# Four chained adaLN blocks on one core: how the first group's bias reaches the Vector engine, and where the later biases are computed

## What is computed

```python
h = gelu(embedding @ W0 + b0); h = gelu(h @ W1 + b1)
att   = softmax(h @ W2 + b2)                       # 64 x 8
agg_w = einsum('bk,koi->boi', att, weight)         # a 32 x 32 matrix for each sample
agg_b = att @ bias_k                               # 64 x 32: the bias
cond  = einsum('boi,bih->boh', agg_w, x) + agg_b[:, :, None]
ffn   = (silu(cond @ W_gate.T) * (cond @ W_up.T)) @ W_down.T      # 512 -> 1792 -> 512
```

## Time and profile before

| what | us |
|---|---|
| median of 3 runs | 540.56 |
| lowest, highest | 539.83, 541.33 |
| the profiled execution, its own time | 541.38 |
| its span (first to last instruction) | 539.5 |
| PE busy in the span | 528.5 (98%) |
| DVE, ACT, POOL busy | 236.1, 140.7, 153.8 |

### The profile page before, as it was taken

How to read it: one execution, slowest core, us unless ns; L and a number is a source line. 1 busy time by engine, 2 the same in 40 slices (tenths; PEclk the granted TensorE clock), 3 DMA queues, 4 the chain that set the end, 5 groups by cost and what they waited for, 6 DMA issues and landing times.

```text
span 539.5 us, 6961 instructions
## 1 busy us (share of the span) xinstructions
PE 528.5 (98%) x2643; PEld 392.4 (73%) x2643; DVE 236.1 (44%) x537; ACT 140.7 (26%) x247; POOL 153.8 (29%) x153
## 2 busy tenths in 40 slices
PE   7999999999999999999999999999999999989997
PEld 6888888888888888888888886635454544567885
DVE  3432343622223623233522334544525257887665
ACT  5422222322222322222222222000002217545333
POOL 3399994400000400000300930040002000127556
PEclk9999999999999999999999999999999999999999
DMA  8298540295000230000305000959696919589763
GB/s 298 98 416 319 176 103 0 74 146 111 0 0 0 85 90 0 0 0 0 94 6 137 1 1 0 149 130 160 198 190 176 229 26 224 110 167 195 186 137 137
DMA packets 82502, 61.60 MB, mean 114 GB/s; under 512 B 61744, under 2 KB 66864, under 8 KB 81712
## 3 DMA queue, kind: packets, MB, share of 16 engines
q1 hardware_dynamic: 77696, 41.83, 35.2%
q0 software_dynamic: 4704, 19.40, 14.2%
q10 hardware_dynamic: 80, 0.08, 0.0%
HBM read 38.98 MB, written 12.81 MB: 96 GB/s over the span
## 4 chain that ended last, share of the span: by engine, by line
PE 94%; DVE 3%; ACT 1%; DMA 1%; issue 0%; POOL 0%; DVEq 0%; POOLq 0%
PE ps L673 93%; DVE cT L1368 1%; DMA pack_a<-in_pack_a 1%; ACT c_hi L1069 0%; PE ps L873 0%; PE ps L834 0%; DVE xs L1194 0%; DVE rest L1385 0%; PE ps L988 0%; PE ps L887 0%; DVE wcat L1391 0%; DVE m L1381 0%; POOL silu L568 0%; DVE cT L1194 0%; DVE stat L1394 0%
## 5 line engine op out<-in xcount | busy, mean ns | idle before, releaser
L673 PE MATMUL ps<-c_hi,wl 128*128 128x512 f32 x448 | 169.9, 389 | 0.0
L673 PE MATMUL ps<-c_lo,wl 128*128 128x512 f32 x448 | 169.7, 389 | 0.0
L1194 DVE TENSOR_TENSOR hff<-silu,ps 128x512 f32<-128x512 f32 x56 | 38.5, 687 | 164.7 <-PE ps L673 164.7
L673 PEld LDWEIGHTS ps<-c_lo,wl 128*128 128x128 f32 x448 | 84.1, 188 | 17.4
L673 PEld LDWEIGHTS ps<-c_hi,wl 128*128 128x128 f32 x448 | 84.0, 188 | 17.4
L673 PE MATMUL ps<-wl,h_hi 128*128 128x512 f32 x224 | 87.7, 391 | 0.0
L673 PE MATMUL ps<-wl,h_lo 128*128 128x512 f32 x224 | 87.2, 389 | 0.0
L1103 ACT ACTIVATE silu<-ps 128x512 f32<-128x512 f32 x56 | 33.5, 598 | 118.6 <-PE ps L673 118.6
L1194 DVE TENSOR_TENSOR h_lo<-hff,h_hi 128x512 fp32r<-128x512 f32 x56 | 46.8, 836 | 39.1 <-ACT h_hi L1069 39.1
L1069 ACT ACTIVATE h_hi<-hff 128x512 fp32r<-128x512 f32 x56 | 35.4, 632 | 108.8 <-DVE hff L1194 108.8
L673 PE MATMUL ps<-wbase,cT 128*128 128x512 f32 x128 | 56.4, 594 | 0.0
(11 more groups left out here) (184 smaller groups left out, 568.3 us busy)
## 6 DMA issues: line engine op xcount, KB each, us to landing
wl<-in_wl POOLq DMA_DIRECT2D x14, 768.0 KB, 8.5
stg<-y_dram SPq DMA_DIRECT2D x64, 128.0 KB, 5.0
xs<-in_x SPq DMA_DIRECT2D x4, 1024.0 KB, 8.2
x_all<-in_x SPq DMA_DIRECT2D x1, 4096.0 KB, 13.7
y_dram<-prod SPq DMA_DIRECT2D x16, 256.0 KB, 2.2
x_dram<-x_all SPq DMA_DIRECT2D x4, 1024.0 KB, 7.0
x_all<-cS POOLq DMA_DIRECT2D x4, 1024.0 KB, 7.6
x_all<-in_bias POOLq DMA_DIRECT2D x4, 1024.0 KB, 10.8
```

What stands on the lines that cost most here:

```text
L673: return pe.matmul(o, l, r, start=start, stop=stop)
L1194: return dve.tensor_tensor(o, a, b, op)
```

## The change

The transpose of the first attention is taken from `att[:, 0]` (64 x 8) as soon as it is normalised, ahead of the three masked products; a small product with `kbias[0:8]` (8 rows, 32 columns) gives the bias of all 64 samples for block 0; ACT copies it to `btab[:, 0]`; SP writes its first 16 rows to a DRAM tensor, waits, and reads them back broadcast into `bias_bc`. Gone are the transpose of `att_m[:, 0]`, the copy to `attT[:, 0]`, `terms`, the wide product and the copy to `bias_bc`, and two of five filler products. POOL issues weight slices 0 and 1 at once, and 2 and 3 after `bias_bc` has landed. The other biases (block 1: 2 matmul instructions; blocks 2 and 3: 4; the bias by rows: 8) move from behind the 16 products to three places inside `gate_up(0, 0)`, ahead of the high pairs of chunks 0, 1 and 2. `gate_up(0, 0)` stands ahead of the loop, and `gate_up(g + 1, 0)` at the end of the loop's body; each group's matmuls and their order stay.

```diff
# SP
+            sp.wait_ge(s_btab0, 1)
+            sp.dma_start(bias0_dram, btab[0:GB, 0]).then_inc(s_bias0_dram, 16)
+            sp.wait_ge(s_bias0_dram, 16)
+            sp.dma_start(bias_bc[:], bias0_dram.rearrange("b o -> (b o)").unsqueeze(0).broadcast_to([P, TOK])).then_inc(s_bias_bc[0], 16)
             sp.wait_ge(s_btab, 2)
             sp.dma_start(bias_dram, btab[:]).then_inc(s_bias_dram, 16)
# POOL
-            weights(0, 3)
+            weights(0, 2)
             pool.wait_ge(s_pack_c, 16)
-            pool.wait_ge(s_attT, 1)
-            pool.tensor_tensor(terms.rearrange("p (b o) -> p b o", o=ROWS),
-                               attT[:, 0, 0:GB].unsqueeze(2).broadcast_to([P, GB, ROWS]),
-                               kbias[:, 0:ROWS].unsqueeze(1).broadcast_to([P, GB, ROWS]), ALU.mult).then_inc(s_terms, 1)
+            pool.wait_ge(s_bias_bc[0], 16)
+            weights(2, 4)
             split_c(0)
-            weights(3, 4)
             pool.wait_ge(s_h_lo, 1)
             weights(4, M)
# PE
             pe.wait_ge(s_set, 2)
-            for n in range(5):
+            for n in range(3):
                 mm(bank(7)[:, 0:P], ones[:], ones[:])
+            pe.wait_ge(s_pack_c, 16)
+            pe.wait_ge(s_att, 6)
+            pe.transpose(bank(0)[0:K, 0:NB], att[:, 0], ident[0:NB, 0:NB]).then_inc(s_first_turned, 1)
             pe.wait_ge(s_att, 7)
             mm(bank(3)[:, 0:NT * K], selrep, att_m[:, 0]).then_inc(s_att_spread, 1)
-            pe.wait_ge(s_pack_c, 16)
-            pe.transpose(bank(0)[:, 0:NB], att_m[:, 0], ident[0:NB, 0:NB]).then_inc(s_att_turned, 1)
+            pe.wait_ge(s_att_first, 1)
+            mm(bank(0)[0:NB, P:P + ROWS], att_first, kbias[0:K, 0:ROWS]).then_inc(s_bias0, 1)
...
-            pe.wait_ge(s_terms, 1)
-            mm(bank(0), ones[:], terms).then_inc(s_bias0, 1)
...
                 if m == 0:
                     for s in range(S):
+                        ahead(s)
                         pe.wait_ge(s_c_hi, S * g + s + 1)
...
             def layer0(g, more):
-                for m in range(M):
+                for m in range(1, M):
                     gate_up(g, m)
-                    if m >= 1 and (more or m < M - 1):
+                    if more or m < M - 1:
                         down(g, m - 1)
...
-            pe.wait_ge(s_attT, 2)
-            for l, i in COND.items():
-                mm(bank(1)[0:NB, l * ROWS:(l + 1) * ROWS], attT[:, i], kbias[:, i * ROWS:(i + 1) * ROWS])
-            mm(bank(1)[0:NB, ROWS:2 * ROWS], condT, cwT)
-            for b in range(TB):
-                ins = mm(bank(1)[b * ROWS:(b + 1) * ROWS, P:P + NT], ...)
-            ins.then_inc(s_bias_mm, 1)
+            pe.wait_ge(s_attT, 1)
+            def later_bias(s):
+                if s == 0:
+                    mm(bank(1)[0:NB, ROWS:2 * ROWS], condT, cwT)
+                elif s == 1:
+                    for l in (2, 3):
+                        i = COND[l]
+                        mm(bank(1)[0:NB, l * ROWS:(l + 1) * ROWS], attT[:, i], kbias[:, i * ROWS:(i + 1) * ROWS])
+                elif s == 2:
+                    for b in range(TB):
+                        ins = mm(bank(1)[b * ROWS:(b + 1) * ROWS, P:P + NT], ...)
+                    ins.then_inc(s_bias_mm, 1)
+            gate_up(0, 0, later_bias)
             with pe.Fori(0, G - 1) as g:
                 layer0(g, True)
+                gate_up(g + 1, 0)
             layer0(G - 1, False)
# ACT
+            act.wait_ge(s_first_turned, 1)
+            copy(att_first, bank(0)[0:K, 0:NB]).then_inc(s_att_first, 1)
+            act.wait_ge(s_bias0, 1)
+            copy(btab[:, 0], bank(0)[0:NB, P:P + ROWS]).then_inc(s_btab0, 1)
             act.wait_ge(s_att_turned, 1)
-            copy(attT[:, 0], bank(0)[:, 0:NB]).then_inc(s_attT, 1)
-            act.wait_ge(s_att_turned, 2)
             copy(attT[:, 1:3].rearrange("p i n -> p (i n)"), bank(1)[:, 0:2 * NB]).then_inc(s_attT, 1)
             act.activation(scrap[:], scrap[:], ACT.Silu)
-            act.wait_ge(s_bias0, 1)
-            copy(bias_bc[:], bank(0)).then_inc(s_bias_bc[0], 16)
```

More of the change, by code:

```diff
@@ L171, in build @@
         bias_dram = nc.dram_tensor("bias_dram", (NB, 4, ROWS), F32).ap()
+        bias0_dram = nc.dram_tensor("bias0_dram", (GB, ROWS), F32).ap()
         ps = ctx.enter_context(nc.psum_tensor("ps", [P, 8, 512], F32))
@@ L213, in cT3 @@
             return xs if g % 2 else cT
-        terms = silu[:, 0]
+        att_first = silu[0:K, 0, 0:NB]
         prod0 = hff[:].rearrange("p b (j k o) -> p (b j) k o", k=K, o=ROWS)
@@ L242, in build @@
         s_attT = sem("s_attT")
-        s_terms = sem("s_terms")
+        s_first_turned = sem("s_first_turned")
+        s_att_first = sem("s_att_first")
         s_bias0 = sem("s_bias0")
+        s_btab0 = sem("s_btab0")
+        s_bias0_dram = sem("s_bias0_dram")
         s_mix0 = sem("s_mix0")
@@ L726, in cond, with gate_up @@
                     cond_chunk(l, g, s, b)
-            def gate_up(g, m):
+            def gate_up(g, m, ahead=lambda s: None):
                 n = g * M + m
@@ L804, in _ @@
                         ins.then_inc(s_cond_mm[0], 1)
-            pe.wait_ge(s_attT, 2)
-            for l, i in COND.items():
-                mm(bank(1)[0:NB, l * ROWS:(l + 1) * ROWS], attT[:, i], kbias[:, i * ROWS:(i + 1) * ROWS])
-            mm(bank(1)[0:NB, ROWS:2 * ROWS], condT, cwT)
-            for b in range(TB):
-                ins = mm(bank(1)[b * ROWS:(b + 1) * ROWS, P:P + NT], kbias[:, COND[2] * ROWS:(COND[2] + 1) * ROWS],
-                         attT[:, COND[2]].rearrange("p (t b) -> p b t", b=TB)[:, b])
-            ins.then_inc(s_bias_mm, 1)
+            pe.wait_ge(s_attT, 1)
[8 more added lines that the diff above has]
+                    for b in range(TB):
+                        ins = mm(bank(1)[b * ROWS:(b + 1) * ROWS, P:P + NT], kbias[:, COND[2] * ROWS:(COND[2] + 1) * ROWS],
+                                 attT[:, COND[2]].rearrange("p (t b) -> p b t", b=TB)[:, b])
+                    ins.then_inc(s_bias_mm, 1)
+            gate_up(0, 0, later_bias)
             with pe.Fori(0, G - 1) as g:
                 layer0(g, True)
+                gate_up(g + 1, 0)
             layer0(G - 1, False)
@@ L1110, in _ @@
             act.wait_ge(s_bias_mm, 1)
-            copy(btab[:].rearrange("b l o -> b (l o)"), bank(1)[0:NB, 0:4 * ROWS]).then_inc(s_btab, 1)
+            copy(btab[:, 1:4].rearrange("b l o -> b (l o)"), bank(1)[0:NB, ROWS:4 * ROWS]).then_inc(s_btab, 1)
             copy(biasN, bank(1)[:, P:P + NT]).then_inc(s_biasN, 1)
```

## The result

The changed kernel is slower: a median of 542.50 us over 19 runs against 541.51 of the kernel before over 19 runs beside it, a ratio of 1.0019 with a 95% interval of 1.0013 to 1.0026. That is 1.0 us where 0.4 less was forecast. It lies inside what the prediction called no change (0.3%), but the interval over 19 runs leaves out 1, and the sign is not the one that was forecast. The median of before in that comparison is 0.95 above the three runs known ahead, so differences count here, not absolute times.

A forecast was written before the change was run, and what follows sets the result against it. The prediction took PE's chain through the beginning, up to gate_up(0, 0), as the bound. An earlier chunk 0 (-0.6) and the moved biases (+0.2) gave -0.4 us, median 540.56 to 540.2, range 539.0 to 542.1.

The forecast's parts named there:

- no change (0.3%): Whole kernel: 0.3%, 1.6 us, can't be told from no change; a result within that had a chance of 0.82.
- PE's path through the beginning: Before 19.2 us: PE's waits decide; any gain or loss reaches the end of block 0, 330.8, unchanged.
- The fillers' step: PE's beginning: four fewer filler instructions end 0.85 us earlier; the spreading product starts at 9.30, all DVE work 0.25 earlier.
- The loop's edge at 0: gate_up(g + 1, 0) ahead of the loop's jump: priced 0, bounds -0.1 and +0.3 us for three edges.
- 22.57: Forecast time at which gate_up(0, 0) is through (slice 1's first product): 16.67 + 5.9, against 22.98 before.
- The profiled execution would take 541.38 - 0.4: Whole kernel: the profiled execution falls to 540.98 us, the median from 540.56 to 540.2.
- The 0.6 of chunk 0 (16.57): The 16 xs products: chunk 0 complete at 16.57, so DVE adds the bias at 16.67, not 17.27, 0.6 us earlier.
- The first rival: Clock rises later: all 32 instructions of the 16 products run low, +1.35 us, up to 2 more; median 542.1; chance 0.12.
- I take 3.0 and 2.6: it lands at 16.3: Bias by DRAM: store 3.0 us, load 2.6, landing at 16.3 against 16.6 when DVE asks, slack 0.3 us.
- I estimate 0.3 for a visit: Each of three later-bias places inside gate_up(0, 0): 0.3 us, plus 0.06 per instruction and 0.07 for the last 8.
- 5.9: From DVE's first addition to the end of gate_up(0, 0): 5.9 us with the moved biases, against 5.7 before.
- A rule stood apart: Bias store and load: about 2.0 us fixed each plus bytes at 436 GB/s, 4.6 us the pair, landing at 15.3.

The follow-up runs named there:

- e2: Changed kernel plus two filler products (4 instructions) behind the small transposes, where PE waits for blk; ratio 1.0013 to the kernel before.
- e1: Changed kernel with bias_bc loaded from other data right behind xs, so DVE never waits for the DRAM trip (bias not right); ratio 1.0016 to the kernel before.
- e3: Changed kernel with the later biases back in one piece behind the 16 products; ratio 1.0009 to the kernel before.
- e4: Kernel before with three filler products at the beginning instead of five, nothing else; ratio 1.0012 to the kernel before.
- f2: Kernel before with three fillers at the beginning instead of five, and two filler products behind PE's last product; ratio 0.9987 to the kernel before.
- f3: Changed kernel with three filler products (6 instructions) as PE's very last; ratio 1.0009 to the kernel before.
- g1: Changed kernel with the later biases back in one piece and three filler products behind PE's last product; ratio 1.0000 to the kernel before.
- g2: g1 with bias_bc loaded from other data right behind xs (bias not right); ratio 0.9994 to the kernel before.
- f1: Kernel before with gate_up(0, 0) ahead of the loop and later biases in three places inside it, wide product kept; ratio 0.9999 to the kernel before.
- f4: Kernel before with five more filler products ahead of PE's first wait for pack_a; ratio 0.9997 to the kernel before.
- h1: f2 with the wide product issued twice; ratio 1.0011 to the kernel before.

## Why the prediction was wrong

**Right.** That PE's path through the beginning decides, and that block 0 behind 19 us absorbs or adds nothing: the window without a gap is as long as before. The fillers' step held to 0.1 us: everything starts 0.12 late here because pack_a landed at 3.67 instead of 3.54, the spreading product comes at 9.41 (9.30 and that 0.12), SP issues at 10.80 (10.67), the first `xs` product at 12.66 (12.47). The loop's edge at 0 held as far as PE has no gap there.

**Wrong, by step.** In the profile slice 1 came at 23.30 instead of 22.57. Of the 0.73 us, 0.12 is pack_a, 0.39 is DVE's start (steps 2 and 3), 0.22 the visits (step 4). Step 1 lies outside the span.

1. "The profiled execution would take 541.38 - 0.4": the text took what lies around the span (1.9 us) as a constant. It is not. The program of PE is six matmul instructions shorter, and one fetch fewer falls inside the span. On one chip the kernels with 14 fetches (before, 35 runs; e2, 11 runs) never spent over 2.0 us outside, those with 13 (e1, e3, e4) did so in 20 of 34 runs; and fillers behind the last product took the excess away in three pairs: e4 and f2 (1.0012 to 0.9987), the changed kernel and f3 (1.0019 to 1.0009), e3 and g1 (1.0009 to 1.0000), each time with the time outside cut from at most 3.0 to at most 1.9. The two halves of each pair ran at different times, of the first and the last on different chips. Share: the time outside gives 0.2 us on the mean for the changed kernel (2.05 against 1.84); the ratios of changed kernel and f3 are 0.5 us apart, with an uncertainty as large.
2. The 0.6 of chunk 0 (16.57) rested on a rise of the clock at the time of one profile. In the changed kernel's own profile the rise came 0.9 later, at the 18th of 32 instructions, and chunk 0 was complete at 17.00. The first rival named the mechanism and gave it 0.12. Whether the change itself delays the rise stays open: kernels with the same beginning differ by as much as 2.1 us in it, and its time follows neither the number of fillers (16.0 with none, 15.75 with five, 16.1 with ten) nor the gap ahead of the products in a way that these runs show. e2, with the gap filled, had the earliest rise of those above, 14.8.
3. "I take 3.0 and 2.6: it lands at 16.3": 3.4 and 3.0, from 10.80, landed at 17.15. DVE would have started no earlier with the clock's rise of before; and with the bias in time it would have started at 17.1, for chunk 0. The two delays stood side by side, and each hid the other. How much the bias costs by itself changes with the rise: 1.1 us in the profile of e2, 0.4 in that of f3, 0.15 in that of the changed kernel, none in e3 and g1. Over all runs g1 and g2 give 0.3 us, with an uncertainty of 0.6: not shown beyond noise.
4. "I estimate 0.3 for a visit": too small, 6.12 - 5.9 = 0.2 in all. The greater error was the comparison: the text set the visits against the piece as it stood on PE's path before, though its own step had brought PE ahead of DVE, where most of the piece costs nothing (g1: 5.65). That holds only where the products end early enough: in e3 and g2, whose products ended at 19.2 and 19.4, the piece took 6.2 as well. Price by f3 and g1: 0.0009, 0.5 us, uncertainty 0.6; the profiles of f1 and before, with equal rises, say 0.6, the medians of these two nothing.

The account in ratios: 1.0019 changed; 1.0009 with the last fetch inside; 1.0000 with the biases in one piece; 0.9994 with a bias in time. Each step is as large as its interval; from 1.0019 to 1.0000 the sum is beyond it, so the fetch and the visits together are shown as the loss, their shares are not. Of the 1.0 us of the medians, 0.3 is in the profiled pair and 0.2 in the time outside; the other 0.5 is not traced to anything. And a gain that is clear of noise, of the removed wide product of 1.87 us, was seen in no version.

A rule stood apart in the prediction: by the Trainium skill, DMA: Bandwidth & Descriptors, Anatomy of one DMA, the pair of transfers was an estimated 4.6 us. The page gives that fit for DMAs that the general engine issues, and SP issued these two; the trace has 6.4 (3.4 and 3.0), and the measurement decides.

Also by the Trainium skill, TensorE: Matmul & The Clock Gate, Part 1, sustained activity releases the half rate; f4 had PE at work from 1.10 on with two short gaps (0.30 and 0.33 us) and saw the low spacing still at 14.15. What else keeps it low no run here shows.

Is there a version that beats both? f2, the kernel before with three fillers at the beginning and two behind the last product, reads 0.9987 (0.9978 to 0.9996), 541.27 against 542.15 beside it. But it is the best of thirteen, e4 does the same work in a span that is not shorter than before's: that it is faster is not shown.

## What to carry to other kernels

When an edit changes the number of instructions, look at the instruction queue of the DMA view near the end, and at time less span in each run: in the kernels with one fetch fewer inside the span, single executions took up to 1.2 us more, 0.2 to 0.5 on the mean, as much as the edit was to bring. When two things release the same step, work out both: the later one sets the time, and making the other faster shows nothing. Before moving work into gaps between dependent steps, ask whether the one wait ahead of them could hold all of it, without changes of shape. And where the matrix engine is still at its low level, one profile is not enough: here the rise moved by up to 2.1 us between executions of the same beginning, and each us of it is half a us of time.

## What the runs showed of the hardware

- A store of 2 KB (16 rows of 128 bytes) beside weight traffic took 3.4 us to land, and a load of 256 KB from one row of 2 KB, alone, 3.0. Over all profiles that have them the store took 2.9 (g1) to 4.7 us (e1), the load 3.0 to 3.2 (g1).
- Time outside the span is 1.8 to 2.0 us for eleven kernels whose last fetch lies inside it, and up to 3.1 for the four others.
- The rise of the clock does not show in the granted clock column, which reads 1.00 from the start; only the spacing of like instructions (0.21 and 0.11 us) tells it. It came between 14.8 (e2) and 18.6 us (g2) in 14 of the 15 profiles, and ahead of the first product, at 15.2, in that of h1.
- A second product of 512 columns right behind a change of shape started 0.35 us behind the first (0.74 - 0.39, changed kernel), against 0.227 in a long row of them.
